# Folding the queries beside the transform in a three-layer kernel of 16 tiles

## The chip, the cores and the metric

The kernel runs on one core of a Trainium2 chip, on which TensorE multiplies matrices, VectorE, ScalarE and GpSimd work element by element, and SyncE only issues DMA transfers. Each engine runs its own list of instructions in order, and engines wait for each other on semaphores. The metric is the device time of one launch in microseconds; lower is better. The time of a kernel here is the median of three runs.

## What is computed

The reference adds three blocks to `x` of shape (64, 32, 256), each on a layer norm of `x`:

```python
# 1: attention over a context of 257 rows per sample, then a modulated convolution over time, and a feed-forward part
scores = einsum("bthd,bghd->bhtg", x_text @ Wq, x_vision @ Wk) / sqrt(DH)     # 4 heads of 32
topv, topi = top_k(scores, 32)                                              # softmax over the 32 largest
c_t = mean over heads of that softmax @ (x_vision @ Wv)
x = layernorm(x_text) * (1 + mod_gate * scale_in) + mod_gate * shift_in       # from c_t @ W_film_in
y = s4d(x)                                                                # FFT convolution along time
xt = x_text + y * (1 + mod_gate * scale_out) + mod_gate * shift_out
xt = xt + gelu(layernorm(xt) @ W1 + b1) @ W2 + b2
return layernorm(xt)
# 2: softmax attention of the 32 tokens of a sample over themselves, with a reshape of its output
# 3: eight experts behind a gate: the two best of eight logits, gelu in each expert
out = einsum("bse,bsed->bsd", gates, expert_out)
```

## The kernel before

**Tiles and stages.** The 64 samples are cut into `NT` = 16 tiles of 4 samples, that is 128 tokens on the 128 partitions. A tile passes through four stages in four successive steps, and there are 18 numbered steps: in step n, stage a works on tile n (scores of the first attention and the choice of the 32 largest), stage b on tile n-1 (weighted mean, modulation, convolution, first half of the feed-forward part), stage c on tile n-2 (second half of the feed-forward part, self-attention), and stage dd on tile n-3 (the experts). Steps 3 to 15 have all four stages. `following` is tile n+1, whose queries are prepared in step n; step 15 is the first without it. All matrices are float32; nearly every matmul row of the trace counts twice what the program issues.

**What sets the order.** Nothing but the text: every engine has a `step(a, b, c, dd)` written out by hand, and an engine does its pieces in that order. `wait(engine, semaphore, tile.count(per, more))` waits until the semaphore has reached per·n + more. `link` in VectorE's program makes the next instruction wait for the end of this one. Inside the feed-forward part and the experts TensorE has its big pieces: `wide` (L1136, eight or sixteen matmuls with 128 columns), `down` (L1159) and `experts` (L1153, L1151).

**Preparing the next queries.** `query(following)` on TensorE (L1089) makes the queries `qT` of the next tile, and ScalarE copies them out (L623). `keyed(following)` (L1099, L1104) folds the key weights into them, head by head: twelve small matmuls that contract over 32 rows and write the two banks of `SS` (heads 0 and 1) and the two of `PC` (heads 2 and 3). ScalarE copies the result to `qk1` and `qk2` (L641), which `scores` (L1116) and `scores_end` (L1122, L1125) read in the next step. `query` stands after the self-attention's scores (L1289), `keyed` between the two halves of `wide` with `w1`.

**The transform of stage b.** VectorE makes `xf` (L913, L914), TensorE transforms it with four small matmuls that also contract over 32 rows (L1254, `fwd_mm`) into `BB[:, :, 0:D]` and `PC[:, :, D:2D]`, VectorE multiplies by the kernel's spectrum into `had` in two operations (L924, L925), and TensorE transforms back (L1264, `inv_mm`).

**The weights of stage a and b.** For each sample VectorE finds and removes the eight largest of 257 values four times (`find8` L811, `take8` L817, and `maxima` and `take` for the first eight), multiplies (`probs`, L825) and inverts the sum (L829). GpSimd turns that inverse into `wsel` (L580), and TensorE's L1201 (`am_mm`) waits for it: it forms the mean over heads.

**The self-attention's softmax** starts with TensorE's L1289 (`s_mm`); VectorE takes the maximum (L952), adds two experts (L850), inverts, scales and transposes (L957 to L960), normalizes `hn` (L963) and adds two more experts. TensorE's L1151 of the last expert term waits for those (`acc_v`). Then come L1316 (`o2_mm`), VectorE's `x2` (L970) and its statistics (L781, L782), and on GpSimd `norm(3)` and `length` (L553 to L569), the weights of stage a (L580), `xt_b` (L607), the result `out_sb` (L612), and, as the first thing of the next step, the weights of stage b (L580).

## Time and profile before

| | |
|---|---|
| median of three runs | 602.14 us (600.91 to 603.63) |
| the profiled execution, in all | 601.02 us |
| its span, first to last instruction | 599.2 us |
| one full step | 31.60 us |
| busy: TensorE / VectorE / ScalarE / GpSimd | 550.1 / 497.5 / 292.6 / 282.3 us |
| granted TensorE clock, mean | 0.972 |

The span is the profiled execution without 1.8 us around it. Steps 4 to 14 repeat to a few hundredths of a microsecond, so one of them stands for all. The rows further down name the step from 361.83 us, where TensorE starts the half of `w1` in step 10, to 393.42 us, where it does the same in step 11; step 15 reaches that place at 519.91 us. In the timeline a piece's start is exact to two digits, while its length contains the modelled end of its last matmul, so pieces are measured here from start to start.

### The profile page before, as it was taken

The page shows a single profiled execution, that of the slowest core. Times are in us where ns is not written, and L with a number is a line of the kernel's source. Part 1 is how long each engine was busy: PE and PEld are TensorE (multiplying, and loading weights), DVE is VectorE, ACT ScalarE, POOL GpSimd, SP SyncE. Part 2 cuts the span into 40 slices and gives each one's busy share as a digit, 9 for nine tenths or more (in the row PEclk, how much of TensorE's full clock was granted, in tenths as well). Part 3 has the DMA queues.
Part 4 walks back from the last instruction along what each step waited for, and adds up shares of the span by engine and source line. Part 5 has one row for each costly group of instructions (what it writes and reads, how often), then busy time and mean ns, then how long its engine had stood idle before and what let it go on. Part 6 is the DMA issues. An engine that isn't in the chain of part 4 may idle for free.

```text
span 599.2 us, 13091 instructions
## 1 busy us (share of the span) xinstructions
PE 550.1 (92%) x4558; PEld 406.0 (68%) x4558; DVE 497.5 (83%) x1761; ACT 292.6 (49%) x768; POOL 282.3 (47%) x662
## 2 busy tenths in 40 slices
PE   2588487999999999999999999999999999989877
PEld 2344264868686877778786868686868687766755
DVE  7997877689898999989899999898999899966433
ACT  3132242364646565555546463646464656434522
POOL 7755147525445362626363636353544535251621
PEclk9998898899999999999999999999999999989988
DMA  8488203030403030301213030303030300000000
GB/s 269 76 311 340 79 1 122 2 113 2 131 2 131 1 128 4 100 33 59 73 25 108 19 113 20 112 19 114 2 131 2 131 1 10 2 10 2 9 1 18
DMA packets 17957, 42.33 MB, mean 71 GB/s; under 512 B 2770, under 2 KB 9570, under 8 KB 17380
## 3 DMA queue, kind: packets, MB, share of 16 engines
q1 hardware_dynamic: 17892, 41.51, 20.7%
q8 instruction: 36, 0.59, 0.4%
q14 instruction: 29, 0.24, 0.1%
HBM read 39.37 MB, written 2.13 MB: 69 GB/s over the span
## 4 chain that ended last, share of the span: by engine, by line
PE 77%; DVE 3%; issue 3%; POOL 3%; ACT 2%; POOLq 0%; DVEq 0%
PE D L1136 9%; PE BB L1136 9%; PE BB L1159 8%; PE D L1153 8%; PE SS L1116 4%; PE SS L1122 3%; PE PC L1277 3%; PE PC L1316 2%; PE PC L1279 2%; PE BB L1237 2%; PE BB L1238 2%; PE BB L1272 2%; PE BB L1271 2%; PE PC L1219 2%; PE BB L1254 2%
## 5 line engine op out<-in xcount | busy, mean ns | idle before, releaser
L553 POOL TENSOR_SCALAR var_in<-mv 128x1 f32<-128x1 f32 x64 | 14.0, 219 | 238.4 <-DVE mv L782 140.9
L817 DVE MATCH_REPLACE8 work<-top,work 128x257 f32<-128x257 f32 x192 | 77.5, 412 | 0.0
L1136 PE MATMUL D<-ang,e_w 128*128 128x128 f32 x512 | 73.6, 292 | 0.0
L1136 PEld LDWEIGHTS D<-ang,e_w 128*128 128x128 f32 x512 | 65.6, 202 | 10.1 <-issue 10.1
L811 DVE MAX8 top<-work 128x8 f32<-128x257 f32 x192 | 71.1, 412 | 0.0
L1153 PE MATMUL D<-expw,ang 128*128 128x256 f32 x256 | 66.0, 389 | 1.2 <-ACT ang L628 0.9
L1136 PE MATMUL BB<-ang,w 128*128 128x128 f32 x512 | 65.0, 282 | 0.9 <-ACT ang L709 0.9
L1136 PEld LDWEIGHTS BB<-ang,w 128*128 128x128 f32 x512 | 62.1, 196 | 3.1 <-ACT ang L709 1.3
L628 ACT ACTIVATE ang<-BB,cols 128x128 f32<-128x128 f32 x128 | 36.5, 367 | 50.9 <-PE BB L1136 50.9
L1159 PE MATMUL BB<-expw,ang 128*128 128x256 f32 x256 | 57.9, 379 | 0.0
L649 ACT ACTIVATE expo<-SS,nmax,srs 128x257 f32<-128x257 f32 x64 | 32.7, 562 | 51.5 <-DVE work L797 51.3
L1153 PEld LDWEIGHTS D<-expw,ang 128*128 128x128 f32 x256 | 45.7, 190 | 12.8 <-issue 4.5
L1159 PEld LDWEIGHTS BB<-expw,ang 128*128 128x128 f32 x256 | 47.4, 190 | 5.8
L850 DVE SCALAR_TENSOR_TENSOR ang<-D,gate,ang 128x256 f32<-128x256 f32 x96 | 41.7, 476 | 1.1 <-PE D L1153 1.1
L1116 PE MATMUL SS<-ctx_t,qk 128*128 128x257 f32 x128 | 35.5, 402 | 7.3 <-ACT expo L649 6.1
L555 POOL TENSOR_TENSOR rstd<-var_in,mhalf 128x1 f32<-128x1 f32 x64 | 36.3, 567 | 5.3
L649 ACT ACT_TABLE_LOAD x28 | 35.9, 1283 | 0.5
L628 ACT ACTIVATE ang<-D,cols 128x128 f32<-128x128 f32 x128 | 35.7, 355 | 0.5 <-PE D L1136 0.3
L1116 PEld LDWEIGHTS SS<-ctx_t,qk 128*128 128x128 f32 x128 | 23.3, 201 | 16.0 <-issue 13.9
L825 DVE SCALAR_TENSOR_TENSOR prob<-work,expo 128x257 f32<-128x257 f32 x64 | 32.6, 546 | 0.0
L580 POOL TENSOR_SCALAR wsel<-head,rsum_row,tm_tile 128x32 f32<-128x32 f32 x64 | 23.6, 380 | 14.5 <-issue 13.1
L790 DVE MAX8 top<-SS 128x8 f32<-128x257 f32 x64 | 23.9, 414 | 4.6 <-PE SS L1125 4.6
(262 smaller groups left out, 1238.5 us busy)
## 6 DMA issues: line engine op xcount, KB each, us to landing
ctx_n<-in_ctx_n SPq DMA_DIRECT2D x16, 768.0 KB, 4.3
ctx_t<-in_ctxT SPq DMA_DIRECT2D x16, 514.0 KB
ctx_t<-in_ctxT SPq DMA_DIRECT2D x16, 257.0 KB
xT<-in_xT SPq DMA_DIRECT2D x16, 128.0 KB, 2.5
x_all<-in_x SPq DMA_DIRECT2D x4, 512.0 KB, 9.2
out<-out_sb SPq DMA_DIRECT2D x16, 128.0 KB, 1.7
ctx_l<-in_ctx_l SPq DMA_DIRECT2D x16, 96.0 KB, 5.1
w<-in_W SPq DMA_DIRECT2D x1, 1024.0 KB
```

Source lines behind the costliest of these rows:

```text
L555: link(tt(rstd[k][:, 0:1], w, mhalf[:, 0:1], ALU.pow))
L628: ins = A(dst[:, k, :], bank[:, 128 * (k % 4):128 * (k % 4) + 128], ACT.Gelu, bias=bias[:, k:k + 1])
L649: A(expo[:, 2 * q + k, :], S[k][:, 0:G], ACT.Exp, bias=nmax[:, 2 * q + k:2 * q + k + 1], scale=srs[:, a.n, 2 * q + k:2 * q + k + 1]).then_ ...
L790: V.max(top[:, 2 * q + k, 0:8], S[k][:, 0:G]).then_inc(chains["top"], 1)
L811: V.max(top[:, 2 * q + k, 8 * r8:8 * r8 + 8], work[:, 2 * q + k, :]).then_inc(chains["top"], 1)
L817: V.match_replace(work[:, 2 * q + k, :], top[:, 2 * q + k, 8 * r8:8 * r8 + 8], work[:, 2 * q + k, :], TAKEN).then_inc(chains["taken"], 1)
L825: V.scalar_tensor_tensor(prob[:, 2 * q + k, :], work[:, 2 * q + k, :], TAKEN, expo[:, 2 * q + k, :], ALU.is_equal, ALU.mult, accum_out=psu ...
L850: V.scalar_tensor_tensor(acc[k % 2][:, :], bank, gate[:, k:k + 1], acc[k % 2][:, :], ALU.mult, ALU.add).then_inc(s["acc_v"], 1)
L1116: MM(S[u][:, 0:G], qk1[:, 2 * q + u, :, :].rearrange("p h t -> p (h t)"), ctx_t1[a.p][:, 2 * q + u, :], start=True, stop=False)
L1136: ins = MM(bank[:, 128 * m:128 * m + 128], w[:, k, at:at + 128], xs[:, 128 * k:128 * k + 128], start=k == 0, stop=k == 1)
L1153: MM(bank, act2[:, k, :], e_w2[:, k, :], start=True, stop=True).then_inc(s["eo_mm"], 1)
L1159: ins = MM(B1[:, 0:D], act1[:, k, :], w2[:, k, :], start=k == 0, stop=k == HID // 128 - 1)
```

## The change

**TensorE.** `query(following)` is issued after stage b's L1219 (`z_mm`) and writes `B1[:, D:2D]` in place of a part of `PC`; it waits for `xt2_v` of stage c. `keyed(following)` is issued right behind the forward transform and writes the unused columns of the `BB` banks in place of `SS`, and `PC` as before. The two halves of `w1` are next to each other. The transform waits for `qT_a` too, and the transform back waits for both parts of ScalarE's copy (`qk_a`).

**ScalarE.** The copy of `qT` stands behind `zT`; the four copies of the folded queries stand behind the gelus of the experts and ahead of the exponentials of the second half of the scores. Heads 2 and 3 come first. A one-element exponential ahead of them asks for the exponential's table. `qk1` and `qk2` have two buffers.

**VectorE.** The first multiplication into `had` waits for `qk_mm`, the second for the first part of `qk_a`. The normalization of stage c goes from three operations to two (`u_c`, `x1`). Chains of dependent operations (statistics, `yb`, `gate`, `logit`) have a `find8`, `take8` or `prob_of` between their links. `sums(b, 1)`, the inverse that `wsel` needs, stands behind `xt2`; `find8(a, 1, 1)` stands ahead of `x2`.

```diff
-        qk1 = sb("qk1", [128, BT, H, T])
+        qk1 = [sb(f"qk1_{i}", [128, BT, H, T]) for i in range(2)]
...
         top = sb("top", [128, BT, TOPK])
         nmax = sb("nmax", [128, BT])
...
+            def keyed(a, low=BB, first=D):
 
                 wait(act, s["qk_mm"], a.count(1, 1))
-                for dst, at, n in ((qk1, 0, BT), (qk2, 128, BT // 2)):
-                    for h, banks in ((0, SS), (2, PC)):
+                wait(act, s["sc_mm"], a.count(4, -4))
+                for h, banks, shift in ((2, PC, 0), (0, low, first)):
+                    if banks is BB:
+                        wait(act, s["had_v"], a.count(2, -3))
+                    for dst, at, n in ((qk1[a.p], 0, BT), (qk2[a.p], 128, BT // 2)):
                         ins = A(dst[:, :, h:h + 2, :].rearrange("p b h t -> p h b t"),
-                                banks[:, :, at:at + T * n].rearrange("p h (b t) -> p h b t", b=n), ACT.Copy)
-                ins.then_inc(s["qk_a"], 1)
+                                banks[:, :, shift + at:shift + at + T * n].rearrange("p h (b t) -> p h b t", b=n), ACT.Copy)
+                    ins.then_inc(s["qk_a"], 1)
...
+                if following:
+                    query(following)
...
                     gelus(act2, 1, D0, e_b1, "e1b_mm", "g2b_a", dd)
+                if following:
+                    A(ahead[:, :], b1[:, 0:1], ACT.Exp)
+                    keyed(following)
...
-                if following:
-                    query(following)
...
-                if following:
-                    keyed(following)
...
                 if b:
-
                     top8(b, 1, 3)
-                    probs(b, 1)
-                if c:
-
+                    prob_of(b, 1, 0)
+                    prob_of(b, 1, 1)
+                if c:
                     wait(dve, s["h2_mm"], one(c))
                     wait(dve, s["xtb_g"], one(c))
                     V.tensor_tensor(xt2[:, :], xt_b[:, :], B1[:, 0:D], ALU.add).then_inc(s["xt2_v"], 1)
+                if b:
+                    sums(b, 1)
+                if c:
                     wait(dve, s["xt2_v"], one(c))
-                    stats(1, xt2[:, :], c, "st1_v")
+                    link(V.bn_stats(bn[1][:, :], xt2[:, :]))
+                    V.bn_aggr(mv[1][:, :], bn[1][:, :]).then_inc(s["st1_v"], 1)
...
                     maxima(a, 0)
+                if c:
+                    wait(dve, s["st1_v"], one(c))
+                    V.scalar_tensor_tensor(u_c[:, :], xt2[:, :], mv[1][:, 0:1], gout[:, :], ALU.subtract, ALU.mult).then_inc(chains["u"], 1)
+                if a:
                     take(a, 0)
...
+                    V.scalar_tensor_tensor(logit[:, :], dots[:, NE:2 * NE], inorm[:, :], dots[:, 0:NE], ALU.mult, ALU.add).then_inc(chains["best"], 1)
+                if a:
+                    find8(a, 0, 1)
...
+                if dd:
+                    wait(dve, chains["best"], dd.count(2, 2))
+                    V.tensor_scalar(nbest[:, :], best[:, 0:1], -1.0, None, ALU.mult).then_inc(s["nbest_v"], 1)
+                if a:
+                    find8(a, 0, 2)
+                if b:
                     wait(dve, s["z_mm"], one(b))
...
                     wait(dve, s["rs1_g"], one(c))
-                    V.tensor_scalar(u_c[:, :], xt2[:, :], mv[1][:, 0:1], rstd[1][:, 0:1], ALU.subtract, ALU.mult).then_inc(chains["u"], 1)
-                if dd:
-                    wait(dve, chains["best"], one(dd))
-                    V.tensor_scalar(nbest[:, :], best[:, 0:1], -1.0, None, ALU.mult).then_inc(s["nbest_v"], 1)
-                if c:
-                    wait(dve, chains["u"], c.count(2, 1))
-                    V.tensor_tensor(u_c[:, :], u_c[:, :], gout[:, :], ALU.mult).then_inc(chains["u"], 1)
-                    wait(dve, chains["u"], c.count(2, 2))
                     wait(dve, s["xb_g"], one(c))
-                    V.tensor_tensor(x1[:, :], u_c[:, :], xb_c[:, :], ALU.add).then_inc(s["x1_v"], 1)
+                    wait(dve, chains["u"], one(c))
+                    V.scalar_tensor_tensor(x1[:, :], u_c[:, :], rstd[1][:, 0:1], xb_c[:, :], ALU.mult, ALU.add).then_inc(s["x1_v"], 1)
...
-                if a:
-                    find8(a, 0, 2)
...
+                if a:
+                    take8(a, 0, 2, (0,))
...
                     wait(dve, s["fwd_mm"], one(b))
+                    if following:
+                        wait(dve, s["qk_mm"], one(following))
...
-                    V.tensor_tensor(had[0:NF, 0:2, :], BB[0:NF, :, 0:D], kern_two, ALU.mult)
+                    V.tensor_tensor(had[0:NF, 0:2, :], BB[0:NF, :, 0:D], kern_two, ALU.mult).then_inc(s["had_v"], 1)
+                    if following:
+                        wait(dve, s["qk_a"], following.count(2, 1))
                     V.tensor_tensor(had[0:NF, 2:4, :], PC[0:NF, :, D:2 * D], kern_two, ALU.mult).then_inc(s["had_v"], 1)
...
-                if a:
-                    take8(a, 0, 2)
...
+                if b:
                     wait(dve, s["y_a"], one(b))
                     wait(dve, s["y_mm"], one(b))
-                    link(V.tensor_tensor(yb[:, :], yb[:, :], B1[:, 0:D], ALU.mult))
-                    link(V.tensor_tensor(yb[:, :], yb[:, :], B1[:, D:2 * D], ALU.add))
+                    V.tensor_tensor(yb[:, :], yb[:, :], B1[:, 0:D], ALU.mult).then_inc(chains["y"], 1)
+                if a:
+                    take8(a, 0, 2, (1,))
+                if b:
+                    wait(dve, chains["y"], b.count(2, 1))
+                    V.tensor_tensor(yb[:, :], yb[:, :], B1[:, D:2 * D], ALU.add).then_inc(chains["y"], 1)
+                if a:
+                    find8(a, 0, 3, (0,))
+                if b:
+                    wait(dve, chains["y"], b.count(2, 2))
                     wait(dve, s["xln_g"], one(b))
                     V.tensor_tensor(xt[:, :], yb[:, :], xln[b.n % 3][:, :], ALU.add).then_inc(s["xt_v"], 1)
+                if a:
+                    find8(a, 0, 3, (1,))
+                if b:
                     wait(dve, s["xt_v"], one(b))
                     link(V.bn_stats(bn[0][:, :], xt[:, :]))
                     V.bn_aggr(mv[0][:, :], bn[0][:, :]).then_inc(s["st0_v"], 1)
-                if a:
-                    find8(a, 0, 3)
-                if c:
-
+                if c:
                     wait(dve, s["s_mm"], one(c))
                     V.reduce_max(nmax_c[:, :], C0[:, D:D + T], AXX, negate=True).then_inc(s["nmaxc_v"], 1)
...
                     take8(a, 0, 3)
+                    find8(a, 1, 1)
                 if c:
                     wait(dve, s["o2_mm"], one(c))
                     V.tensor_tensor(x2[c.p][:, :], x1[:, :], C0[:, 0:D], ALU.add).then_inc(s["x2_v"], 1)
+                if a:
+                    prob_of(a, 0, 0)
+                if c:
                     wait(dve, s["x2_v"], one(c))
-                    stats(3, x2[c.p][:, :], c, "st3_v")
-                if a:
-                    probs(a, 0)
-                    top8(a, 1, 1)
+                    V.bn_stats(bn[3][:, :], x2[c.p][:, :]).then_inc(chains["bn3"], 1)
+                if a:
+                    prob_of(a, 0, 1)
+                if c:
+                    wait(dve, chains["bn3"], one(c))
+                    V.bn_aggr(mv[3][:, :], bn[3][:, :]).then_inc(s["st3_v"], 1)
+                if a:
+                    sums(a, 0)
+                    take8(a, 1, 1)
...
+            def query(a, bank=B1):
 
...
-                    ins = MM(PA[:, D:D + 128], wq[:, k, :], xT[a.p][:, k, :], start=k == 0, stop=k == 1)
...
+                    ins = MM(bank[:, D:D + 128], wq[:, k, :], xT[a.p][:, k, :], start=k == 0, stop=k == 1)
                 ins.then_inc(s["qT_mm"], 1)
...
+            def keyed(a, low=BB, first=D):
 
                 wait(pe, s["qT_a"], a.count(1, 1))
-                wait(pe, s["mr1_v"], a.count(4, 0))
-                wait(pe, s["exp_a"], a.count(4, 0))
-                for h, bank in enumerate((S[0], S[1], PA, C0)):
+                if low is SS:
+                    wait(pe, s["mr1_v"], a.count(4, 0))
+                    wait(pe, s["exp_a"], a.count(4, 0))
+                banks = (low[:, 0, first:first + DV], low[:, 1, first:first + DV], PA[:, 0:DV], C0[:, 0:DV])
+                for h, bank in enumerate(banks):
                     rows = slice(DH * h, DH * h + DH)
...
-                wait(pe, s["qk_a"], a.count(1, 1))
+                wait(pe, s["qk_a"], a.count(2, 2))
...
+                if following:
+                    if c:
+                        wait(pe, s["xt2_v"], one(c))
+                    if a.n == 1:
+                        pe.wait_ge(s["kt_sb"], 1)
+                    query(following)
...
+                    if following:
+                        wait(pe, s["qT_a"], one(following))
...
                     ins.then_inc(s["fwd_mm"], 1)
+                if following:
+                    if c:
+                        wait(pe, s["x2_v"], c.count(1, 0))
+                    keyed(following)
...
-                    wait(pe, s["had_v"], one(b))
+                    wait(pe, s["had_v"], b.count(2, 2))
+                    if following:
+                        wait(pe, s["qk_a"], following.count(2, 2))
...
-                if following:
-                    if dd:
-                        wait(pe, s["gT_a"], one(dd))
-                    query(following)
...
-                if following:
-                    if c:
-                        wait(pe, s["x2_v"], one(c))
-                    keyed(following)
```

`top8` is still `find8` and `take8`, and `probs` is now `prob_of(a, q, 0)`, `prob_of(a, q, 1)` and `sums(a, q)`; `chains` has four more names. The two tiles prepared before the first step use `PA` and `SS` as before.

On TensorE, from the self-attention's scores (L1289; L1341 in the change) to the feed-forward part with `w1`. Before, with `query` (L1089) and the start of `keyed` (L1099, L1104):

```order
L1289 MATMUL PC<-ang 32x32 x8
L1089 MATMUL PC<-xT1,head 128x128 x2
L1153 MATMUL D1<-expw,ang 128x256 x2
L1153 MATMUL D0<-expw,ang 128x256 x2
L1305 MATMUL PC<-ang,pT_blk 32x64 x16
L1082 MATMUL BB<-head,ang 128x128 x2
L1151 MATMUL D1<-e_b2,gateT 128x256
L1316 MATMUL PC<-wvo,ang 128x256 x2
L1136 MATMUL BB<-ang,w1 128x128 x8
L1099 MATMUL SS<-qT,head 128x128 x2
L1099 MATMUL PC<-qT,head 128x128 x2
L1104 MATMUL SS<-qT,head 64x64 x2
```

The change, from the same place:

```order
L1341 MATMUL PC<-ang 32x32 x8
L1191 MATMUL D1<-expw,ang 128x256 x2
L1191 MATMUL D0<-expw,ang 128x256 x2
L1353 MATMUL PC<-ang,pT_blk 32x64 x16
L1118 MATMUL BB<-head,ang 128x128 x2
L1189 MATMUL D1<-e_b2,gateT 128x256
L1364 MATMUL PC<-wvo,ang 128x256 x2
L1174 MATMUL BB<-ang,w1 128x128 x16
L1197 MATMUL BB<-expw,ang 128x256 x8
```

Query and fold have left this stretch, and the sixteen matmuls with `w1` (L1174) are one piece.

On TensorE, where the query has gone, from the mean's product with the context (L1257) to the transposes of `z` (L1270, L1271), in the change:

```order
L1257 MATMUL PC<-ctx_n1,amT 32x192 x8
L1125 MATMUL BB<-xT1,head 128x128 x2
L1174 MATMUL D0<-ang,e_w1 128x128 x4
L1270 MATMUL PC<-head,z 128x128
L1271 MATMUL PC<-head,z 64x128
```

And where the fold has gone, from the experts' gate (L1285) on, in the change; L1300 is the transform, L1137 and L1142 are the fold:

```order
L1285 MATMUL PC<-head,gate 8x128
L1154 MATMUL SS<-ctx_t1_0,qk1_0 128x257 x2
L1300 MATMUL BB<-ang,cols 96x256 x2
L1300 MATMUL PC<-ang,cols 96x256 x2
L1137 MATMUL BB<-qT,head 128x128 x2
L1137 MATMUL PC<-qT,head 128x128 x2
L1142 MATMUL BB<-qT,head 64x64 x2
L1142 MATMUL PC<-qT,head 64x64 x2
```

Four more rows of L1142 follow, then L1160 (before: L1122), which stood right behind the transform.

On ScalarE, from the copies of `zT` to the exponentials. Before:

```order
L678 ACTIVATE zT1<-PC 128x128
L679 ACTIVATE zT2<-PC 64x128
L628 ACT_TABLE_LOAD
L628 ACTIVATE ang<-D1,cols 128x128 x4
L623 ACTIVATE gateT<-PC 8x128
L628 ACTIVATE ang<-D0,cols 128x128 x4
L649 ACT_TABLE_LOAD
L649 ACTIVATE expo<-SS,nmax,srs 128x257 x2
```

The change, in which L623 copies `qT`, L691 is the one-element exponential and L644 the fold's copies:

```order
L681 ACTIVATE zT1<-PC 128x128
L682 ACTIVATE zT2<-PC 64x128
L623 ACTIVATE qT<-BB 128x128
L628 ACT_TABLE_LOAD
L628 ACTIVATE ang<-D1,cols 128x128 x4
L623 ACTIVATE gateT<-PC 8x128
L628 ACTIVATE ang<-D0,cols 128x128 x4
L691 ACT_TABLE_LOAD
L691 ACTIVATE ahead<-cols 128x1
L644 ACTIVATE qk1_1<-PC 128x2x4x32
L644 ACTIVATE qk2_1<-PC 128x2x2x32
L644 ACTIVATE qk1_1<-BB 128x2x4x32
```

The table load that stood ahead of `expo` stands ahead of the fold's copies, and one copy stands ahead of the gelus' table load.

On VectorE, from `x2` (L970; L998 in the change) on. Before:

```order
L970 TENSOR_TENSOR ang<-ang,PC 128x256
L781 BN_STATS bn3<-ang 128x6
L782 BN_AGGR mv3<-bn3 128x2
L825 SCALAR_TENSOR_TENSOR prob,psum_row<-work,expo 128x257 x2
L829 RECIPROCAL rsum_row<-psum_row 128x2
L811 MAX top<-work 128x8 x2
L817 MATCH_REPLACE work<-top,work 128x257 x2
```

The change:

```order
L810 MAX top<-work 128x8 x2
L998 TENSOR_TENSOR ang<-ang,PC 128x256
L823 SCALAR_TENSOR_TENSOR prob,psum_row<-work,expo 128x257
L1003 BN_STATS bn3<-ang 128x6
L823 SCALAR_TENSOR_TENSOR prob,psum_row<-work,expo 128x257
L1008 BN_AGGR mv3<-bn3 128x2
L830 RECIPROCAL rsum_row<-psum_row 128x2
L816 MATCH_REPLACE work<-top,work 128x257 x2
```

L1003 and L1008 are the statistics of `x2`; each has one L823 ahead of it, and the search of eight (L810) has gone ahead of `x2`.

## Rows read from the trace of the kernel before

**Rows 1.** The page, costliest groups: line, engine, operation, count | busy, mean ns | idle.
```profile
L811 DVE MAX8 top<-work 128x8 f32<-128x257 f32 x192 | 71.1, 412 | 0.0
```

**Rows 2.** Windows: start:end, length, busy PE, PEld, DVE, ACT, POOL, clock, DMA, GB/s.
```profile
361.83:372.28 10.45, 10.45 (x90) 8.92 (x88) 10.04 (x39) 3.54 (x13) 7.23 (x19) 1.00 0.04 13
372.28:383.23 10.95, 10.95 (x88) 7.50 (x87) 9.58 (x35) 8.71 (x20) 6.42 (x14) 1.00 0.48 166
383.23:388.51 5.28, 5.28 (x31) 3.42 (x30) 5.11 (x19) 2.23 (x6) 0.27 (x2) 1.00 0.01 3
388.51:392.02 3.51, 3.51 (x63) 2.82 (x63) 3.17 (x13) 2.25 (x6) 1.33 (x4) 1.00 0.02 5
519.91:530.37 10.46, 8.03 (x55) 7.25 (x54) 10.05 (x39) 2.85 (x10) 7.30 (x19) 1.00 0.04 13
515.01:518.51 3.50, 3.43 (x59) 2.28 (x58) 3.15 (x13) 2.11 (x5) 1.30 (x4) 1.00 0.03 7
```

**Rows 3.** Timeline of TensorE: start, length, line, operation, out<-in, shapes, count, idle before.
```profile
361.83 1.95 PE L1136 MATMUL BB<-ang,w 128*128 128x128 f32 x16
...
363.71 0.38 PE L1099 MATMUL SS<-qT,head 32*128 32x128 f32 x2
...
364.44 2.05 PE L1136 MATMUL BB<-ang,w 128*128 128x128 f32 x16
...
388.80 0.71 PE L1089 MATMUL PC<-xT,head 128*128 128x128 f32 x4
...
389.34 1.89 PE L1153 MATMUL D<-expw,ang 128*128 128x256 f32 x8
...
519.91 3.73 PE L1136 MATMUL BB<-ang,w 128*128 128x128 f32 x32
...
530.37 0.64 PE L1201 MATMUL PC<-prob,wsel 128*32 128x257 f32 x8 [1.96 <-POOL wsel L580]
```

**Rows 4.** Timeline of VectorE, one full step.
```profile
362.03 0.42 DVE L970 TENSOR_TENSOR ang<-ang,PC 128x256 f32<-128x256 f32 x1 [0.87 <-PE PC L1316]
...
362.94 0.18 DVE L782 BATCH_NORM_AGGREGATE mv<-bn 128x2 f32<-128x6 f32 x1
...
371.09 0.17 DVE L829 RECIPROCAL rsum_row<-psum_row 128x2 f32<-128x2 f32 x1
...
382.18 0.68 DVE L925 TENSOR_TENSOR had<-PC,kern_f 96x512 f32<-96x512 f32 x1
...
388.96 0.19 DVE L952 TENSOR_REDUCE nmax_c<-PC 128x1 f32<-128x32 f32 x1 [0.24 <-PE PC L1289]
...
391.10 0.87 DVE L850 SCALAR_TENSOR_TENSOR ang<-D,gate,ang 128x256 f32<-128x256 f32 x2
```

**Rows 5.** Timeline of GpSimd across the boundary of two steps.
```profile
363.22 0.32 POOL L553 TENSOR_SCALAR var_in<-mv 128x1 f32<-128x1 f32 x1 [4.67 <-DVE mv L782]
...
369.85 0.91 POOL L612 TENSOR_TENSOR out_sb<-ang 128x256 f32<-128x256 f32 x1
...
371.42 0.71 POOL L580 TENSOR_SCALAR wsel<-head,rsum_row,tm_tile 128x32 f32<-128x32 f32 x2 [0.66 <-issue]
```

**Rows 6.** Timeline of ScalarE in the same step.
```profile
365.09 0.41 ACT L641 ACTIVATE qk<-PC 128x256 f32<-128x256 f32 x1
...
377.27 0.28 ACT L678 ACTIVATE zT<-PC 128x128 f32<-128x128 f32 x1
...
377.72 1.28 ACT L628 ACT_TABLE_LOAD   x1
...
379.01 1.14 ACT L628 ACTIVATE ang<-D,cols 128x128 f32<-128x128 f32 x4
...
381.29 1.28 ACT L649 ACT_TABLE_LOAD   x1
```

**Rows 7.** Landing of the transposed tokens of tile 2, issued at 41.7 us.
```profile
DMA to landing us min/median/max: 15.4/15.4/15.4
```

**Rows 8.** Timeline of VectorE, last step but one.
```profile
563.71 0.41 DVE L887 TENSOR_SCALAR ang<-ang,mv,rstd 128x256 f32<-128x256 f32 x1 [1.41 <-POOL rstd L408]
```

More of the change, by code:

```diff
@@ L165, in build @@
         am = sb("am", [128, G])
-        qk2 = sb("qk2", [128, BT // 2, H, T])
+        qk2 = [sb(f"qk2_{i}", [128, BT // 2, H, T]) for i in range(2)]
         top = sb("top", [128, BT, TOPK])
@@ L276, in build @@
         s = {n: sem(n) for n in names}
-        chains = {n: sem("self_" + n) for n in "tm g0 g1 g2 g3 len top taken u xhat best".split()}
+        chains = {n: sem("self_" + n) for n in "tm g0 g1 g2 g3 len top taken u xhat best y gate bn2 bn3".split()}
         ld_x = [sem(f"ld_x{k}") for k in range(4)]
@@ L728, in _ @@
             first = Tile(0)
-            query(first)
-            keyed(first)
+            query(first, PA)
+            keyed(first, SS, 0)
             exps(first, 0)
@@ L802, in top8, with find8 @@
                 take8(a, q, r8)
-            def find8(a, q, r8):
-                for k in range(2):
+            def find8(a, q, r8, ks=(0, 1)):
+                for k in ks:
                     if r8 == 1:
@@ L829, in probs @@
                 V.reciprocal(rsum_row[:, 2 * q:2 * q + 2], psum_row[:, 2 * q:2 * q + 2]).then_inc(s["rsum_v"], 1)
+            def probs(a, q):
+                prob_of(a, q, 0)
+                prob_of(a, q, 1)
+                sums(a, q)
             def step(a, b, c, dd):
@@ L1121, in scores_end @@
                     rows = slice(64 * u, 64 * u + 64)
[L1122 removed]
+                    MM(S[u][:, 0:G], qk2[a.p][rows, q, :, :].rearrange("p h t -> p (h t)"), ctx_t2[a.p][rows, q, :], start=False, stop=False)
                 for u in range(2):
@@ L1344, in _ @@
             pe.wait_ge(s["wqc_v"], 1)
-            query(first)
-            keyed(first)
+            query(first, PA)
+            keyed(first, SS, 0)
             pe.wait_ge(s["fills"], N_FILLS)
```

58 lines of the change are left out of this document (29 added, 29 removed).

## The prediction

> **What bounds the kernel now.** I read four views, in this order. The page first: TensorE is the busiest engine and VectorE is close behind it, so either can be what a step waits for. Then the windows of one full step, cut at the places where TensorE meets another engine [rows 2]: from 361.83 us, A to the mean over heads (10.45 us), B to the transform back (10.95), C to the self-attention's scores (5.28), D to the last expert term (3.51), and E, what is left of 31.60 until the next 361.83 (1.41). TensorE is busy for all of A to D, which looks like a step that only TensorE's work can shorten or lengthen. The third view corrects that. Step 15 prepares no further tile, so it runs D without the query and the stretch A that follows without the fold. D still takes 3.50 and A still takes 10.46, now with TensorE busy for only 8.03 of it [rows 2], and 1.96 us of idle time ahead of L1201 ended by GpSimd's `wsel` [rows 3]. So in A and D TensorE and the others arrive together: 0.54 us of query in D (388.80 to 389.34) and 0.73 us of fold in A (363.71 to 364.44) [rows 3] fill time in which TensorE would otherwise wait. The fourth view, the engines' timelines, says for whom. In D it is VectorE: L952 at 388.96 and its work behind it, until the second L850 ends at 391.10 + 0.87 = 391.97; TensorE's L1151 starts at 392.02 [rows 2, 4]. In A it is the way from `x2` at 362.03 over VectorE to the inverse at 371.09 [rows 4], over GpSimd's weights at 371.42 to L1201 at 372.28 [rows 2, 5]. Step 16's A has the same 1.96 us waiting at its end, for the same reason.
>
> **The change part by part, for one full step.** The change takes the query out of D and the fold out of A and puts both into B, where TensorE has no such slack.
>
> Piece B holds what is added: 10.95 + 0.54 + 0.73 = 12.2 if TensorE alone sets it. But the second multiplication into `had` now needs ScalarE's copies, and TensorE's transform back stands behind that wait, with everything after it. ScalarE's list from `zT` on has no gap today: 377.27 to 381.29, 4.0 us, with one table load in it [rows 6]. It starts 5.0 us after L1201 (372.28), and 5.5 with the query ahead of it. The copy of `qT` adds about 0.2 (like `zT`'s first copy, 0.28, overlapped by the next). Then 1.28 for the exponential's table, which is only moved ahead of the copies, 0.1 to 0.2 for the one-element exponential, about 0.6 for the copies of heads 2 and 3 (0.41 for the first, rows 6, and a half-sized one), and 0.68 for L925 [rows 4]: 5.5 + 4.0 + 0.2 + 1.3 + 0.15 + 0.6 + 0.7 = 12.45, and 12.5 with a semaphore. I take 12.5. The bounds are 12.1, if the copies come in time and the fold costs a little less beside the transform, and 12.9, if ScalarE is held up once more. Today L925 is done at 382.86, 0.37 ahead of TensorE, so that wait is new.
>
> The load is where a rule speaks against the change. In the trace the load at 377.72 takes 1.28 us and the gelu follows at 379.01 [rows 6]. The Trainium skill, "ScalarE: Activation LUTs", section "What ACT_TABLE_LOAD costs", puts 1.38 us of draining on top of a load of 1.28; the row agrees on the load and shows no drain behind it. With the drain the wait would be 1.4 us longer in each of 12 steps, some 17 us more than my sum.
>
> Piece C keeps its work. ScalarE's exponentials and its copy for L1277 follow VectorE's next maxima, which follow `had`, so all of it shifts with the new wait: 5.3 (5.3 to 5.5).
>
> Piece D loses 0.54 us of TensorE's work and none of VectorE's between L952 and the second L850; nothing is woven in there. Step 15 has shown what that is worth: nothing. In addition `hn`, which stands ahead of that L850, gets its statistics later, because the chain from `yb` on now has a `take8` and two `find8` in it, three operations of 0.37 [rows 1] that replace gaps of some 0.1 each. I add 0.1: 3.6 (3.5 to 3.8).
>
> Piece A loses the fold: TensorE would be at L1201 after 9.5 (0.73 less, and 0.2 because 32 matmuls in one piece take 3.73 against 1.95 + 2.05 for two halves [rows 3]). VectorE gets there sooner as well: two searches of 0.37 [rows 1] are done while it waits 0.87 for `x2` [rows 4], and gaps are filled, so its 9.06 us from `x2` to the inverse become some 8. That leaves GpSimd. It starts when the statistics of `x2` are there (362.94, GpSimd at 363.22) and works without a gap until 369.85 + 0.91 = 370.76 [rows 4, 5]; only then comes the weights' turn. Two multiplications now stand inside those statistics, about 0.35 each, of which some 0.25 fill gaps: 0.45 later. From 361.83 that is 1.4 + 0.45 + 7.5 = 9.35 us, and 0.86 from the weights' start to L1201 (371.42 to 372.28): 10.2. Some of GpSimd's pieces should be shorter, since they meet other work of VectorE than today (`out_sb` takes 0.91 beside a multiplication of VectorE), so I take 10.1. Bounds: 9.5, and 10.7 if they get longer, or if `xt2`, now ahead of the inverse, waits for `xt_b`.
>
> Piece E stays at 1.4. The sum is 10.1 + 12.5 + 5.3 + 3.6 + 1.4 = **32.9, against 31.6: 1.3 us more**, twelve times (steps 3 to 14): 15.6. With all lower bounds it is 31.8, or 0.2 more; with all upper ones 34.3.
>
> **The edges.** In steps 1 and 2 TensorE waits a lot, so the query is nearly free; but `xT` of tile 2 landed 15.4 us after its issue at 41.7 [rows 7], at 57.1, and I reckon the new query to be up about 0.7 us ahead of that. `had` comes 0.7 later in each and the fold is gone behind `hn`, which cancels; the longer chain to `hn` and a search ahead of `z` add about 1 each. Together 2.6 (0 to 4). At the end, L1201 of step 16 comes 0.3 sooner, and in step 17 the normalization behind 563.71 [rows 8] has one operation less and the gate's are out of its way: together 1.0 sooner. Two buffers for the folded queries cost nothing: no instruction is added. The `sem` and `chains` entries likewise.
>
> **Total.** 15.6 + 2.6 - 1.0 = 17.2. The profiled execution took 601.02 us and would take 618.2; the median of the three runs before is 602.14, 1.1 higher, which gives **619.3**.
>
> **The rivals.**
> First, the waits nearly close: the copies are in time and GpSimd is quick enough. Then each step costs 0.2 and the edges 1.6: 602.1 + 2.4 + 1.6 = 606. For it: every wait above is below 0.6 us and rests on sums of ten small pieces. Against it: D's 0.54 is not in doubt.
> Second, faster: TensorE's work does set the step. D's and A's equality with step 15 would be chance, and the fold beside the transform saves the 0.2 us by which two halves of `w1` are longer than one piece: 602.1 - 12 x 0.2 - 1 = 598.7. Against it: two stretches of step 15 agree with the full step to 0.01 us. The Trainium skill, "TensorEngine Tiling (Array Packing)", section "Key Properties", says that a change of tiling mode drains TensorE, and the fold has the transform's mode; the 0.2 agrees with that, though no row separates the drain from the rest.
> Third, worse: VectorE and GpSimd get in each other's way in A, and ScalarE is late for both `had` and L1277. At the upper bounds 12 x 2.7 + 1.6 = 34: 636. It decides from where `xt2` waits for `xt_b`, since the inverse stands behind it and the weights behind that.
>
> **How the numbers follow.** The forecast, 612 to 626, has 0.63. The first rival, 603 to 609, has 0.15, a third of it within 0.5% (3.0 us, about what a measurement of this kernel can tell from no change). The third, from 626 up, has 0.13, the second 0.06. The remaining 0.03 are no change, from errors both ways. So faster 0.06, same 0.08, slower 0.86. The range from 607 to 630 leaves out the second, two thirds of the first and a third of the third: 0.2.
>
> **What would show it.** In the profile of the change: D as long as before, with idle time ahead of an expert's matmul (L1191, L1189); idle time on TensorE ahead of the transform back (L1316), ended by L947; A between 9.9 and 10.4, ended by `wsel`; GpSimd without a gap from the statistics to the weights. I am wrong if D is near 3.0, if A is at 9.5, or if the full step stays at 31.6.

## The result and the profile after

The kernel after takes **620.16 us** (median of four runs, 619.6 to 621.31), the kernel before beside it 602.88 (600.91 to 605.47). The ratio is **1.029, 95% interval 1.0263 to 1.0317**: slower, by 17.3 us. The profiled execution took 620.5 us with a span of 618.7. Of all executions named below, one (604.48 us, of the kernel with the query ahead) was in a slower state, and the ratios leave it out.

Windows of one full step of the kernel after, cut as in [rows 2], and the A that answers to the one from 519.91 us there (the same columns):

```profile
377.82:388.26 10.44, 9.58 (x65) 8.31 (x64) 8.92 (x39) 2.85 (x10) 7.36 (x19) 1.00 0.01 2
388.26:400.60 12.34, 12.00 (x116) 8.60 (x116) 8.88 (x34) 9.76 (x25) 6.69 (x14) 1.00 0.47 157
400.60:406.01 5.41, 5.41 (x30) 3.34 (x30) 4.89 (x18) 2.23 (x6) 0.00 (x0) 1.00 0.01 3
406.01:409.52 3.51, 3.44 (x59) 2.29 (x58) 3.08 (x13) 2.11 (x5) 1.61 (x5) 1.00 0.00 0
542.24:552.68 10.44, 8.03 (x55) 7.26 (x54) 8.89 (x37) 2.85 (x10) 7.42 (x19) 1.00 0.00 2
```

With E (1.40) the step takes 33.10 us in place of 31.60. B has grown by 1.39 and C by 0.13; A and D, out of which the work was taken, have the length of before to 0.01 us, and TensorE is now busy for 9.58 of A's 10.44. The A from 542.24 us has still less work on TensorE, 8.03 us, and the same length: TensorE doesn't set it.

TensorE's timeline, the rows that answer to [rows 3]:

```profile
388.26 0.64 PE L1239 MATMUL PC<-prob,wsel 128*32 128x257 f32 x8 [0.87 <-POOL wsel L580]
...
391.84 0.71 PE L1125 MATMUL BB<-xT,head 128*128 128x128 f32 x4
...
400.60 0.64 PE L1316 MATMUL BB<-had,dft_y 96*32 96x256 f32 x8 [0.34 <-DVE had L947]
...
406.30 2.33 PE L1191 MATMUL D<-expw,ang 128*128 128x256 f32 x8
```

Where the fold stood TensorE waits 0.87 us for the weights. Where the query stood it spreads the same expert matmuls (eight rows) over 2.33 us in place of 1.89 [rows 3]. And it waits 0.34 us ahead of the transform back. ScalarE, VectorE and GpSimd show for what (answering to [rows 6, 4 and 5]):

```profile
397.89 1.28 ACT L691 ACT_TABLE_LOAD   x1
399.18 0.20 ACT L691 ACTIVATE ahead<-cols 128x1 f32<-128x1 f32 x1
399.29 0.53 ACT L644 ACTIVATE qk<-PC 128x256 f32<-128x256 f32 x2
399.71 0.55 ACT L644 ACTIVATE qk<-BB 128x256 f32<-128x256 f32 x2
401.85 1.02 ACT L652 ACTIVATE expo<-SS,nmax,srs 128x257 f32<-128x257 f32 x2 [1.58 <-DVE work L796]
```

```profile
386.75 0.42 DVE L870 TENSOR_TENSOR ang<-ang,BB 128x256 f32<-128x256 f32 x1 [1.29 <-POOL ang L607]
387.08 0.16 DVE L830 RECIPROCAL rsum_row<-psum_row 128x2 f32<-128x2 f32 x1
...
399.86 0.69 DVE L947 TENSOR_TENSOR had<-PC,kern_f 96x512 f32<-96x512 f32 x1 [0.54 <-ACT qk L644]
```

```profile
379.64 0.19 POOL L553 TENSOR_SCALAR var_in<-mv 128x1 f32<-128x1 f32 x1 [4.54 <-DVE mv L1008]
...
382.96 0.50 POOL L407 TENSOR_SCALAR var_in<-var_in 128x1 f32<-128x1 f32 x1
...
384.68 1.27 POOL L580 TENSOR_SCALAR wsel<-head,rsum_row,tm_tile 128x32 f32<-128x32 f32 x2
385.92 0.72 POOL L607 TENSOR_TENSOR ang<-ang,rows 128x256 f32<-128x256 f32 x1
386.60 0.73 POOL L612 TENSOR_TENSOR out_sb<-ang 128x256 f32<-128x256 f32 x1
387.41 0.71 POOL L580 TENSOR_SCALAR wsel<-head,rsum_row,tm_tile 128x32 f32<-128x32 f32 x2
```

The copies wait for a table load that they don't need, while the exponentials that need it wait another 1.58 us for VectorE. `xt2` (L870) waits 1.29 us for `xt_b`, the inverse stands behind it, and the second weights come last on a GpSimd that has had no gap since 379.64. On the page a search takes 414 ns, against 412 in [rows 1]:

```profile
L810 DVE MAX8 top<-work 128x8 f32<-128x257 f32 x192 | 72.9, 414 | 0.0
```

### The profile page after: what moved, and what is told of

It is laid out like the page before. It is cut to its first block and busy times, and to the rows that moved or that the text cites. A ratio compares the mean times of both kernels' runs of the same rounds, so it can differ in the third digit from the quotient of the medians.

```text
span 618.7 us, 13130 instructions
## 1 busy us (share of the span) xinstructions
PE 552.8 (89%) x4558; PEld 404.0 (65%) x4558; DVE 476.2 (77%) x1745; ACT 294.6 (48%) x782; POOL 287.1 (46%) x662
## 5 line engine op out<-in xcount | busy, mean ns | idle before, releaser
L810 DVE MAX8 top<-work 128x8 f32<-128x257 f32 x192 | 72.9, 414 | 0.0
L1191 PE MATMUL D<-expw,ang 128*128 128x256 f32 x256 | 70.4, 398 | 2.1 <-ACT ang L628 1.0
L1174 PE MATMUL D<-ang,e_w 128*128 128x128 f32 x512 | 71.4, 286 | 0.0
L1174 PEld LDWEIGHTS D<-ang,e_w 128*128 128x128 f32 x512 | 64.7, 199 | 6.5 <-issue 6.5
L1174 PEld LDWEIGHTS BB<-ang,w 128*128 128x128 f32 x512 | 61.5, 197 | 2.1 <-ACT ang L715 1.3
L1174 PE MATMUL BB<-ang,w 128*128 128x128 f32 x512 | 61.7, 280 | 0.9 <-ACT ang L715 0.9
L1191 PEld LDWEIGHTS D<-expw,ang 128*128 128x128 f32 x256 | 44.7, 189 | 18.4 <-DVE ang L856 7.5
L856 DVE SCALAR_TENSOR_TENSOR ang<-D,gate,ang 128x256 f32<-128x256 f32 x96 | 41.6, 475 | 1.1 <-PE D L1191 1.1
L580 POOL TENSOR_SCALAR wsel<-head,rsum_row,tm_tile 128x32 f32<-128x32 f32 x64 | 30.1, 480 | 10.2 <-issue 7.8
L930 DVE TENSOR_TENSOR ang<-xhat,BB 128x256 f32<-128x256 f32 x16 | 6.7, 421 | 33.9 <-PE BB L1282 33.9
L623 ACT ACTIVATE ang<-D 128x256 f32<-128x256 f32 x16 | 6.1, 383 | 43.6 <-PE D L1118 43.6
```

Source lines behind the costliest of these rows:

```text
L580: nc.gpsimd.tensor_scalar(wsel[:, k, :], sel[:, :], rsum_row[:, k:k + 1], tm_tile[:, k:k + 1], ALU.mult, ALU.mult).then_inc(s["wsel_g"], 1)
L810: V.max(top[:, 2 * q + k, 8 * r8:8 * r8 + 8], work[:, 2 * q + k, :]).then_inc(chains["top"], 1)
L856: V.scalar_tensor_tensor(acc[k % 2][:, :], bank, gate[:, k:k + 1], acc[k % 2][:, :], ALU.mult, ALU.add).then_inc(s["acc_v"], 1)
L1174: ins = MM(bank[:, 128 * m:128 * m + 128], w[:, k, at:at + 128], xs[:, 128 * k:128 * k + 128], start=k == 0, stop=k == 1)
L1191: MM(bank, act2[:, k, :], e_w2[:, k, :], start=True, stop=True).then_inc(s["eo_mm"], 1)
```

## The experiments

"The weave" below is VectorE's new program, in which searches and multiplications stand between the links of its chains; "the moves" are those of query and fold on TensorE and ScalarE. Ratios are to the kernel before, run beside each. All piece lengths come from one profile per kernel.

The theory: the loss is work moved out of two places where it cost nothing. What A and D lose comes back as idle time; what B gains is paid. The rivals: VectorE's new order loses it; or TensorE's work as such does.

All pieces named A to E below were read off TensorE's timeline, by the same cuts, in a regular full step.

**Filling the two places again.** The change, with the query and the fold computed once more at their old places, results unused (`folded` holds the matmuls of `keyed` and none of its waits):

```diff
+                if following and dd:
+                    wait(pe, s["had_v"], b.count(2, 2))
+                    for k in range(2):
+                        MM(PA[:, D:D + 128], wq[:, k, :], xT[following.p][:, k, :], start=k == 0, stop=k == 1)
                 if dd:
                     experts(range(4, 6))
...
                     wide(0, B1, w1, hT, "w1a_mm")
+                if following and dd:
+                    wait(pe, s["qT_a"], one(following))
+                    wait(pe, s["mr1_v"], a.count(4, 4))
+                    wait(pe, s["exp_a"], a.count(4, 4))
+                    wait(pe, s["qk_a"], following.count(2, 2))
+                    wait(pe, s["x2_v"], one(c))
+                    folded(SS, 0)
```

> The changed kernel with work repeated, none left out: in each full step TensorE computes the query once more at its old place among the attention's waits, and the fold once more at its old place between the halves of w1, results unused; about 1.2 us more of matrix work per step. My theory: both old places lie in time in which TensorE now waits anyway (0.87 us for GpSimd's weights, some 0.4 us among the attention's experts), so the time stays within 619 to 624 us. Rival, TensorE's own work sets the step: 12 times 1.2 us more, 632 to 636 us.

Measured: 621.56 us (620.83 to 621.85), ratio to before 1.0289 (1.0265 to 1.0312), the change's own ratio. The full step takes 33.10 us again. Windows of A, B and D:

```profile
378.16:388.61 10.45, 10.45 (x90) 8.92 (x88) 8.92 (x39) 2.66 (x9) 7.37 (x19) 1.00 0.00 2
388.61:400.94 12.33, 11.99 (x116) 8.59 (x116) 8.87 (x34) 9.95 (x26) 6.68 (x14) 1.00 0.48 157
...
406.36:409.86 3.50, 3.50 (x63) 2.81 (x62) 3.07 (x13) 2.00 (x5) 1.61 (x5) 1.00 0.00 0
```

TensorE is busy for 0.87 us more in A and fills D, and no time passes for it. Both places are free, as the theory has it, and TensorE's work as such isn't the limit of A and D.

**The moves without the weave, and the weave without the moves.** One kernel is the change with VectorE's old program, the other the kernel before with the new one. The edit is the exchange of VectorE's program, with these waits added to the old one:

```diff
                     wait(dve, s["fwd_mm"], one(b))
+                    if following:
+                        wait(dve, s["qk_mm"], one(following))
...
-                    V.tensor_tensor(had[0:NF, 0:2, :], BB[0:NF, :, 0:D], kern_two, ALU.mult)
+                    V.tensor_tensor(had[0:NF, 0:2, :], BB[0:NF, :, 0:D], kern_two, ALU.mult).then_inc(s["had_v"], 1)
+                    if following:
+                        wait(dve, s["qk_a"], following.count(2, 1))
                     V.tensor_tensor(had[0:NF, 2:4, :], PC[0:NF, :, D:2 * D], kern_two, ALU.mult).then_inc(s["had_v"], 1)
```

> The changed kernel with VectorE's old program (only the waits for the moved fold added). My theory: the moves of query and fold carry the loss: 618 to 624 us, full step about 33.1 us: w1 to mean over heads about 10.4, from there to the inverse transform about 12.4 or a little more, D 3.5. Rival, the weave loses: 602 to 606 us.

Measured: 619.69 us (618.38 to 621.41), ratio 1.0261 (1.0231 to 1.0291), full step 33.1 us, a few a little longer: A 10.45, B 12.34, C 5.41, D and E 4.92. TensorE waits the same 0.88 and 0.34 us in A and B. The moves alone are the loss.

> The kernel before, with the change's VectorE program alone (fused and woven step); query, fold and exponential table stay where they were, one buffer of folded queries. My theory: the loss sits in TensorE's moved work, so this alone gives 600 to 604 us, full step 31.4 to 31.7 us, and the first row of L1239's successor still about 10.45 us behind the start of w1. Rival, the weave is what loses (the second half's reciprocal behind xt2, which waits for GpSimd's xt_b, makes the stretch from w1 to the mean over heads longer): 608 to 620 us.

Measured: **608.27 us** (606.7 to 611.58), ratio 1.0082 (1.0044 to 1.012). That is 4 us above my range and at the lower edge of the rival's, but the place is not the rival's: A stays 10.44. Windows of A to C, and of D with E:

```profile
368.25:378.69 10.44, 10.44 (x89) 8.91 (x88) 8.92 (x38) 3.54 (x13) 7.37 (x19) 1.00 0.00 1
378.69:389.89 11.20, 11.18 (x89) 7.54 (x88) 9.20 (x35) 8.71 (x20) 6.63 (x14) 1.00 0.51 172
389.89:395.17 5.28, 5.28 (x31) 3.42 (x31) 4.48 (x16) 2.23 (x6) 0.00 (x0) 1.00 0.01 4
395.17:400.27 5.10, 5.07 (x69) 4.07 (x69) 4.67 (x18) 3.26 (x8) 1.71 (x5) 1.00 0.02 3
```

B is 0.24 us longer than before and D with E 0.19. VectorE's rows, first of this kernel, then of the kernel before, show the first:

```profile
382.34 0.74 DVE L806 MAX8 top<-work 128x8 f32<-128x257 f32 x2
383.00 0.39 DVE L900 SCALAR_TENSOR_TENSOR z<-ctx_l,am,PC 128x192 f32<-128x192 f32 x1
```

```profile
376.02 0.41 DVE L884 SCALAR_TENSOR_TENSOR z<-ctx_l,am,PC 128x192 f32<-128x192 f32 x1 [0.34 <-PE PC L1219]
```

Behind w1's start `z` comes at 14.75 us in place of 14.19, since a pair of searches has been put ahead of it. In D and E a search among the steps to `hn` does the same. So the weave costs 0.4 us a step by itself. Inside the change this does not add up. As I read it, the query stands there as cover ahead of `z`'s transposes, and the 0.34 us of waiting ahead of the transform back covers the rest. The step from 510.22 us of the change, whose B has neither query nor fold, bears this out: there B is 11.21 and D with E 5.09, so both losses are back.

**The table behind the copies.**

```diff
                 if following:
-                    A(ahead[:, :], b1[:, 0:1], ACT.Exp)
                     keyed(following)
+                    A(ahead[:, 1:2], b1[:, 0:1], ACT.Exp)
```

> The changed kernel with the one-element exponential (and so the table load of 1.28 us) behind the four copies of the fold instead of ahead of them. My theory: the copies end 1.3 us earlier, the wait of 0.34 us before the inverse transform goes in each of some 14 steps, the table is still there before the exponentials (which wait 1.58 us for VectorE): 614 to 617 us. Rival, the wait is only pushed on (exponentials, yb or the scores' maxima come late): 619 to 621 us, nothing changes.

Measured: 616.64 us (614.89 to 617.1), ratio 1.0203 (1.0177 to 1.023). Full step 32.75: B 11.93 with TensorE busy throughout, C back at 5.28, D with E up from 4.91 to 5.10. So 0.41 and 0.13 were gained and 0.19 given back, which is the weave's second loss, now uncovered. ScalarE's rows:

```profile
395.98 0.55 ACT L644 ACTIVATE qk<-PC 128x256 f32<-128x256 f32 x2 [0.69 <-PE PC L1142]
396.77 0.55 ACT L644 ACTIVATE qk<-BB 128x256 f32<-128x256 f32 x2 [0.24 <-DVE had L944]
397.34 1.28 ACT L692 ACT_TABLE_LOAD   x1
398.63 0.20 ACT L692 ACTIVATE ahead<-cols 128x1 f32<-128x1 f32 x1
398.74 1.00 ACT L652 ACTIVATE expo<-SS,nmax,srs 128x257 f32<-128x257 f32 x2
```

**GpSimd's order.** The first weights go ahead of `length`, the second ahead of `out_sb`, and the second inverse back ahead of `xt2`:

```diff
-                if b:
-                    weights(b, 1)
...
                     norm(3, c)
-                    length(c)
                 if a:
                     weights(a, 0)
+                if c:
+                    length(c)
...
                     nc.gpsimd.tensor_tensor(xt_b[:, :], xt[:, :], b2[:, :], ALU.add).then_inc(s["xtb_g"], 1)
+                if a:
+                    weights(a, 1)
...
                     prob_of(b, 1, 1)
+                    sums(b, 1)
...
-                if b:
-                    sums(b, 1)
```

> The changed kernel with GpSimd's order alone corrected (and VectorE's reciprocal for the second half back in front of xt2): the first weights (128x32, two rows of L580) go ahead of the length's chain, the second ones ahead of out_sb. Theory: the 0.87 us for which TensorE waits at the mean over heads is GpSimd's order, so that stretch falls from 10.44 to about 9.6 us, the full step from 33.1 to about 32.2 us, 14 steps: 606 to 611 us. Rival, the wait is pushed to the next one on the path (xt2, logits, z, hn): 615 to 621 us.

Measured: 616.39 us (615.02 to 617.56), ratio 1.0226 (1.0177 to 1.0276): the rival's range. A falls from 10.44 to 9.73, so GpSimd's order did set it, but B rises from 12.34 to 12.69, since TensorE now meets `z` in its late place. In three of the full steps it waits for `xT` besides, with B up to 13.3:

```profile
384.05 0.64 PE L1239 MATMUL PC<-prob,wsel 128*32 128x257 f32 x8 [0.15 <-POOL wsel L580]
...
388.66 0.57 PE L1125 MATMUL BB<-xT,head 128*128 128x128 f32 x3 [0.96 <-DMA xT<-in_xT]
```

SyncE issues `xT` behind the store of `out_sb`, for which it waits, and TensorE is now at the query 2.7 us after that issue (387.70 after 385.01), where it was 4.1 us in the change (391.84 after 387.74). In most steps 2.7 us are just enough. In two of the three with a wait the issue itself lasts 1.7 or 1.81 us in place of 0.43; why isn't shown:

```profile
384.62 0.34 SPq L341 DMA_DIRECT2D out<-out_sb  x1
385.01 1.81 SPq L334 DMA_DIRECT2D xT<-in_xT  x1
```

**Both, and the old order with both.**

> The corrected GpSimd order and the table load behind the fold's copies together. Theory: the two gains add up (0.87 and 0.34 us a step): full step 31.8 to 32.0 us, 602 to 607 us, so no better than the kernel before, because VectorE's woven order still delays z and the last experts by some 0.4 us a step against the kernel before. Rival, they overlap or something else comes late: 608 to 614 us.

Measured: 612.27 us (611.06 to 613.66), ratio 1.0159 (1.0111 to 1.0208); full step 32.4 to 33.2: A 9.73, B from 12.28, C 5.29, D with E 5.10. The rival's number again. A's 0.71 is kept, but B gains only 0.06 on the change: it is 0.35 longer than with the table's move alone, just as it grew by 0.35 with GpSimd's order alone, and in four full steps TensorE waits up to 1.16 us for `xT` on top.

> The moved query and fold, corrected GpSimd order, table load behind the copies, but VectorE's program in its old order. Theory: TensorE then runs without a gap; its work is that of the kernel before less what the fold saves beside the transform (some 0.1 to 0.2 us): full step 31.4 to 31.6 us, 597 to 602 us. Rival, the fold's moved copies on ScalarE or VectorE's old order leave waits at the inverse transform: 603 to 607 us.

Measured: 605.48 us (604.62 to 611.35), ratio 1.0063 (1.0033 to 1.0092); full step 32.01 in its regular form, and up to 32.75 where TensorE waits for `xT`. A is 9.90, B 11.93, C 5.28, D with E 4.91. I missed again, by 3.5 us, and by B: in its regular form, with every wait there gone, it is still 0.97 longer than before, 0.55 of it the query. D has not given that back. I had put the query down as paid by the saving of the fold; it isn't.

> The kernel before with GpSimd's corrected order alone. In the kernel before, the mean over heads starts 10.45 us behind w1, the same as in every kernel so far, with or without the fold (0.73 us) in front of it. Theory: with the fold there, TensorE's own work fills the stretch to within 0.05 us, so nothing changes: 600 to 604 us. Rival, GpSimd sets that stretch here too: the stretch falls to 9.7 to 10.2 us, 594 to 599 us.

Measured: 600.45 us (597.31 to 602.45), ratio 0.9954 (0.992 to 0.9987). The full step is 31.58 with A at 10.43: with the fold in it, TensorE's own work fills A, as expected. The small gain lies where there is no fold: from the w1 that answers to 519.91 us to the next one it takes 31.01 us in place of 33.21, with A at 9.90 in place of 10.46. So in the kernel before GpSimd's order and TensorE's work ended together in A, to 0.02 us.

**The query back in D, one tile ahead.** This is the kernel above (the moves, VectorE's old order, GpSimd's order and the table). The fold stays beside the transform, its query is made in D of the step before (in step 1 it stays where it was), and `xT` is asked for a tile earlier. TensorE's part:

```diff
-                if following:
+                if following and a.n == 1:
...
                     query(following)
...
+                if later:
+                    if dd:
+                        wait(pe, s["gT_a"], one(dd))
+                    query(later, PA)
                 if dd:
                     experts(range(4, 6))
```

> As e7_old_step (fold beside the transform, GpSimd's corrected order, table load behind the copies, VectorE's old order), but the query goes back to its old place among the attention's waits, one tile further ahead (so its result is there for the next step's fold), and SyncE asks for xT one tile earlier. Theory: the query's 0.55 us there is hidden as in the kernel before, the stretch from mean over heads to inverse transform falls from 11.93 to 11.38 us, the waits for xT (0.2 to 0.7 us in four steps) go: full step about 31.5 us, 595 to 600 us. Rival, the stretch with the attention gets as much longer as the other gets shorter: 603 to 606 us.

Measured: **599.39 us** (595.23 to 604.48), ratio 0.9956 (0.9926 to 0.9987), full step 31.57. Windows of A to C, and D with E:

```profile
331.31:341.21 9.90, 9.57 (x66) 8.32 (x65) 9.50 (x39) 2.85 (x10) 6.28 (x18) 1.00 0.00 1
341.21:352.69 11.48, 11.48 (x112) 8.15 (x112) 10.01 (x35) 8.71 (x23) 6.97 (x15) 1.00 0.52 170
352.69:357.98 5.29, 5.29 (x32) 3.34 (x31) 5.12 (x20) 3.33 (x8) 0.25 (x2) 1.00 0.01 3
357.98:362.88 4.90, 4.90 (x70) 4.06 (x69) 3.92 (x15) 3.26 (x8) 1.35 (x4) 1.00 0.00 0
```

B falls by 0.45 us and D with E doesn't move (4.91 and 4.90): the query is free in D and costs 0.45 in B. The waits for `xT` are gone.

But the full step is no shorter than that of the kernel before with GpSimd's order alone (31.58), and the two ratios, 0.9956 and 0.9954, are the same. TensorE has less to do, and waits instead: it is busy for 9.57 of A's 9.90, which is also A's length in that other kernel where the fold is missing. So with VectorE's old order what there is to gain comes from GpSimd's order, and moving the fold has bought nothing.

The same with the woven order, `z` ahead of the searches and the last search behind the moments of `xt`:

> As e9_query_ahead, but with the change's woven VectorE program, two of its rows exchanged: z ahead of the second round's maxima, the last maxima behind the moments of xt. Theory: the woven order gives the probabilities' sums earlier (first stretch 9.7 us instead of 9.9), and with z and hn ahead its loss of 0.4 us a step is gone: full step 31.2 to 31.4 us, 592 to 597 us. Rival, woven order keeps a loss at z or hn: 598 to 604 us.

Measured: **597.09 us** (596.04 to 604.61), ratio **0.9921 (0.9895 to 0.9947)**: faster than the kernel before by 0.8%, which is clear of the noise but small. The step is 31.54, not the 31.2 to 31.4 that I had expected: A is 9.73, D with E 4.90, so the exchange behind `xt` did what it should, but B is 11.62, as I read it since `z` still comes a little late (4.20 us behind L1201's place, against 3.86 in the kernel above). Its step is only 0.03 us shorter than that of the kernel above, so the 2.3 us between the two medians isn't explained by it, and the two intervals overlap. Its interval also overlaps that of GpSimd's order alone. The profiled execution, 601.46 us, was the second slowest of its twelve.

## Why the prediction was right

The forecast was 619.3 us (607 to 630), the result 620.16. Its parts:

- **D** (3.6 forecast, 3.51 measured). Right in its mechanism, and the sign that it names is there: ahead of L1191 TensorE or its weight load stands idle until VectorE's L856 is done, 16 times and 7.5 us in all, where the kernel before has 4 times and 1.9 us (L1153, L850). Moreover, without the query it has the same length, and the kernel that fills the places and the one with the query back in D show the place to be free. The 0.1 for the longer way to `hn` was there in the weave alone (0.19 in D and E), but covered in the change.
- **B** (12.5; 12.34). Right: the wait ahead of the transform back, ended by L947, is there with 0.34 us. The sum over ScalarE was 0.16 too long. The load ahead of the copies costs the 0.41 us of B that moving it behind them returned. The 1.38 us of draining that the prediction names from the Trainium skill, "ScalarE: Activation LUTs", section "What ACT_TABLE_LOAD costs", isn't in the rows: `ahead` follows at 399.18, 1.29 us after the load's start.
- **C** (5.3; 5.41), within its bounds.
- **A** (10.1; 10.44). The step that failed in size was "so I take 10.1". The multiplications among the statistics put GpSimd's start at 1.82 us behind w1, as reckoned (1.4 + 0.45). But GpSimd's list did not get shorter: the first weights took 1.27 us in place of 0.71 and one L407 0.50 in place of 0.34, while `out_sb` saved 0.18 and the smallest pieces some more; in all it is 7.69 us long (379.64 to 387.33), against 7.54 (363.22 to 370.76). (The 0.37 that the prediction gives a search is half a row of two; [rows 1], which it cites, has 412 ns.) And `xt2` did wait for `xt_b`, which I had named as the third rival's deciding point; its price was small, since GpSimd itself, not the inverse, was last. TensorE's 9.5 without the fold was right (9.58 busy). So A gave back nothing of 0.87 us, where I had counted on 0.35.
- **The sum of a step**: 1.50 us more instead of 1.3. Over twelve steps, from the w1 at 112.95 to that at 510.22 us (before: 108.03 to 488.26), it is 397.27 us against 380.23, so 17.0 in place of 15.6. Twelve times 1.50 would be 18.0, but the first of them took 32.48 us in the kernel before, 0.9 more than a regular one.
- **The edges.** In the two profiles step 2's w1, with which the twelve steps begin, starts 4.9 us later (112.95 against 108.03), not 2.6, and what lies behind the twelve steps is 2.5 us shorter, not 1.0. But 4.1 of the 4.9 us arise in the setup, ahead of any work that the change moves. These are TensorE's fold for tile 1, made before the first step, in the kernel before and in the kernel after:

```profile
42.01 0.38 PE L1099 MATMUL SS<-qT,head 32*128 32x128 f32 x2 [1.55 <-ACT qk_w L742]
```

```profile
46.15 0.38 PE L1137 MATMUL SS<-qT,head 32*128 32x128 f32 x2 [1.56 <-ACT qk_w L746]
```

  In the profiles of the other kernels it starts at 42.0 to 42.1 (weave only, GpSimd's order, old order with both) or 45.2 to 46.4 us (the rest, among them the kernel before with GpSimd's order), so it doesn't go with the change. That it differs between executions of one kernel is likely, but not shown, since each has one profile. Behind it the first w1 comes after 32.0 us, against 32.2 before, and the stretch from there to the next w1 takes 1.0 more: 0.8 in place of 2.6. Where the setup ends early (GpSimd's order alone), the same stretch takes 34.5, since `xT` isn't there yet. The 2.5 us at the end are the weave's: from step 16's w1 to the end the kernels with it take 42.6 to 43.7 us, those without it 45.0 to 46.2. The one profile therefore shows 19.5 us of difference and the medians 17.3. My sum was made of 15.6, 2.6 and -1.0; the profiles without that 4.1 give 17.0, 0.8 and -2.5. The total was nearer than its terms: the steps were put 1.4 too low, the start 1.8 too high and the end 1.5 too high, and the setup shifts the profiles by more than any of these. That 619.3 lies within 1 us of 620.16 is in part luck; the range and the mechanism of A to D are not.

The first rival (606) falls with A and B as they were. The second (598.7) was wrong for this change, but its small mechanism is real: TensorE is busy for 31.24 us of a full step with the query back in D, and for 31.60 before, 0.36 less with the fold beside the transform (A 0.88 less, B 0.53 more). No run turned this into time: the full step was 31.57 with it and 31.58 without, both with GpSimd's new order.

## What to carry to other kernels

An engine that is busy throughout a stretch isn't thereby its limit: look for a step that lacks the work in question, or put the work in twice, and see whether the length moves. Work that fills a wait is free where it stands and costs time where the engine has no wait to fill: the query cost nothing in D and 0.45 us in B. Before moving work, try the order of the engine that sets the wait: GpSimd's alone gave as much as the best kernel with the old VectorE order and the moves. An action done "ahead" on an in-order engine is only free if nothing that someone waits for stands behind it: the copies stood behind the table load, and ScalarE was then idle for 1.58 us before the exponentials for which the table was loaded.

## What the runs showed of the hardware

GpSimd's short operations took much longer at some places beside VectorE's work. The pair of L580 takes 1.27 us at 384.68, where VectorE runs its multiplications with a sum (L823, 384.69 to 385.46), and 0.71 at 387.41. With GpSimd's order changed other operations fall beside VectorE's. These are rows of GpSimd, then of VectorE, in the kernel with GpSimd's order changed:

```profile
379.48 0.77 POOL L566 TENSOR_TENSOR var_in<-mv,mhalf 128x1 f32<-128x1 f32 x1
...
381.17 0.92 POOL L568 TENSOR_SCALAR var_in<-rstd,var_in 128x1 f32<-128x1 f32 x1
```

```profile
379.43 0.40 DVE L863 TENSOR_SCALAR ang<-ang,mv,rstd 128x256 f32<-128x256 f32 x1
...
381.19 0.41 DVE L824 SCALAR_TENSOR_TENSOR prob<-work,expo 128x257 f32<-128x257 f32 x1
```

In the kernel after the same two take 0.57 and 0.34 us. A column of 128 values (L568) costs 0.58 us more by its place alone, and reordering GpSimd moved the price to other operations rather than removing it. Which side pays differs: in the kernel before, the multiplication that meets `out_sb` takes 0.94 us and `out_sb` 0.91 [rows 5]:

```profile
370.11 0.94 DVE L825 SCALAR_TENSOR_TENSOR prob<-work,expo 128x257 f32<-128x257 f32 x1
```

That the two engines hold each other up is read from operations that overlap in time; what in VectorE's work does it was not tried.

The setup of 42 or 45 to 46 us, with the same text, is the other thing that I hadn't expected: starts and totals of single profiles compare only behind a common mark.
